# Graph network with gated units on Trainium2: two blocks of the first sum converted ahead of the third layer's weights, and the first normalising blocks placed behind z

## The reference

```python
h = x
for i in range(4):
    hw = einsum('bnc,cd->bnd', h, weight[i])
    m = einsum('bjn,bjd->bnd', adj, hw)
    gx = m @ w_ih[i].T + b_ih[i]
    gh = h @ w_hh[i].T + b_hh[i]
    r = sigmoid(xr + hr);  z = sigmoid(xz + hz)
    n = tanh(xn + r * hn)
    h = (1.0 - z) * n + z * h
y = x + h * mask[:, :, None]
out = (y - mean(y)) / sqrt(var(y) + 1e-5)      # per node, over 128 features
```

## Time and profile before

| | us |
|---|---|
| median of 3 runs | 538.66 (538.38 to 539.0) |
| the profiled execution | 537.98 |
| its span, first to last instruction | 536.2 |
| PE busy in the span | 514.1 (96%), 2288 matmuls |
| DVE busy | 386.1 (72%) |
| ACT busy | 384.6 (72%) |
| POOL busy | 221.2 (41%) |
| granted TensorE clock, mean | 0.990 |

### The profile page before, as it was taken

The page is one execution under the profiler, slowest core; times in us unless marked ns, Lnnn a source line. Parts: engine busy times, 40 slices in busy tenths (PEclk is TensorE's granted clock), DMA queues, the critical chain, the costliest instruction groups (busy, mean ns, idle before and its releaser), DMA issues.

```text
span 536.2 us, 7420 instructions
## 1 busy us (share of the span) xinstructions
PE 514.1 (96%) x2288; PEld 421.5 (79%) x2288; DVE 386.1 (72%) x678; ACT 384.6 (72%) x638; POOL 221.2 (41%) x162
## 2 busy tenths in 40 slices
PE   6999999999999999999999999999999999999970
PEld 4688888888888888888888888888888888888760
DVE  3787666666788886666689886567688887667585
ACT  4668777749776788856886877984986777985444
POOL 2045232344345454432336554232355454344443
PEclk9999999999999999999999999999999999999996
DMA  8941553255732356273662256356472165524212
GB/s 307 382 190 53 213 194 138 91 165 156 238 136 80 122 185 224 82 226 111 198 246 82 65 205 215 117 169 183 137 274 80 60 216 174 185 74 146 90 60 82
DMA packets 78896, 85.13 MB, mean 159 GB/s; under 512 B 3768, under 2 KB 61712, under 8 KB 78864
## 3 DMA queue, kind: packets, MB, share of 16 engines
q1 hardware_dynamic: 78864, 84.73, 47.5%
HBM read 64.27 MB, written 20.45 MB: 158 GB/s over the span
## 4 chain that ended last, share of the span: by engine, by line
PE 92%; DMA 1%; POOL 1%; DVE 1%; issue 1%; SPq 1%; ACT 1%; POOLq 0%; DVEq 0%; ACTq 0%
PE p_S L508 40%; PE p_r L518 6%; PE p_r L522 5%; PE p_r L519 5%; PE p_z L518 5%; PE p_z L522 5%; PE p_z L519 5%; PE p_hn L518 3%; PE p_hn L522 3%; PE p_hn L519 3%; PE p_xn L522 3%; PE p_xn L519 3%; PE p_xn L518 3%; DMA adj_in<-in_adj_dram 1%; PE p_S L478 1%
## 5 line engine op out<-in xcount | busy, mean ns | idle before, releaser
L1272 POOL TENSOR_TENSOR work<-hT,work 128x512 f32<-128x512 f32 x63 | 87.9, 1395 | 266.8 <-ACT work L710 266.8
L508 PE MATMUL p_S<-adj_hi,nat_hi 128*128 128x512 f32 x480 | 187.4, 390 | 0.0
L508 PE MATMUL p_S<-adj_hi,nat_lo 128*128 128x512 f32 x480 | 186.8, 389 | 0.0
L508 PEld LDWEIGHTS p_S<-adj_hi,nat_hi 128*128 128x128 f32 x480 | 90.1, 188 | 18.9 <-DVE nat_lo L894 0.3
L508 PEld LDWEIGHTS p_S<-adj_hi,nat_lo 128*128 128x128 f32 x480 | 90.1, 188 | 18.5
L1141 DVE SCALAR_TENSOR_TENSOR work<-p_hn,bias,work 128x512 f32<-128x512 f32 x62 | 46.5, 750 | 76.2 <-ACT work L710 76.0
L1276 POOL TENSOR_TENSOR work<-work 128x512 f32<-128x512 f32 x63 | 90.1, 1430 | 4.9
L710 ACT ACTIVATE work<-p_r,bsum 128x512 f32<-128x512 f32 x63 | 43.3, 687 | 56.9 <-PE p_r L522 56.2
L931 DVE STREAM_TRANSPOSE work<-hT 128x512 f32<-128x512 f32 x62 | 69.1, 1115 | 2.1
L710 ACT ACTIVATE work<-work,bias 128x512 f32<-128x512 f32 x63 | 45.7, 726 | 31.6 <-DVE work L1145 29.0
L682 ACT ACTIVATE low_words<-adj_in 128x1024 bf16<-128x1024 uint16 x64 | 67.0, 1047 | 1.0
(11 more groups left out here) (148 smaller groups left out, 923.8 us busy)
## 6 DMA issues: line engine op xcount, KB each, us to landing
adj_in<-in_adj_dram SPq DMA_DIRECT2D x72, 512.0 KB, 6.7
bounce<-work SPq DMA_DIRECT2D x62, 256.0 KB, 2.0
low<-bounce SPq DMA_DIRECT2D x62, 256.0 KB, 2.8
x_in<-in_x_dram SPq DMA_DIRECT2D x8, 512.0 KB, 6.8
y<-in_x_dram SPq DMA_DIRECT2D x8, 512.0 KB, 4.4
out_dram<-y SPq DMA_DIRECT2D x7, 512.0 KB, 4.1
out_dram<-y SPq DMA_DIRECT2D x2, 256.0 KB, 2.8
y<-in_L_gnn_w_ih_dram SPq DMA_DIRECT2D x2, 192.0 KB, 7.5
```

The costliest lines, as they stand in the source:

```text
L508: last = nc.tensor.matmul(p_S[h][:, :], part[:, s, j], adj_hi[:, s, j, half(h)], start=(j == 0 and part is nat_hi), stop=(j == NB - 1 and ...
L1272: nc.gpsimd.tensor_tensor(t_sb[:, h], hT[:, s, half(h)], n_sb[:, h], ALU.subtract).then_inc(d_sub, 1)
```

## The change

Three moves, nothing added or removed. On ACT, at the start, the conversion of adjacency block 6 goes from behind `split_joined(2)` to in front of it. On DVE, at the start, `split_weights(2)` goes from in front of `take_odd(0, 7)` to behind `copy_weights(3)`. On ACT, in steps 3 and 4 of pairs 1 to 3, blocks 0 and 1 of the normalising go from `fill(0)` to `fill(1)`.

```diff
                         if g in (3, 4) and not first:
-                            blocks = (range(0, 2), range(0), range(2, 5), range(5, NB))[n]
+                            blocks = (range(0), range(0, 2), range(2, 5), range(5, NB))[n]
                             if len(blocks):
                                 normalise(p - 1, g - 3, blocks)
...
             split_w_hh(1)
             split_joined(1)
             split_w_hh(2)
+            take_adj(0, 0, 6, True)
             split_joined(2)
-            take_adj(0, 0, 6, True)
             split_w_hh(3)
...
             take_odd(0, 5)
             copy_weights(2)
             split_weights(1)
-            split_weights(2)
             take_odd(0, 7)
             copy_weights(3)
+            split_weights(2)
             take_rows()
```

## The result

The changed kernel runs in 537.25 us (median of 21 runs), the kernel before in 538.84 us beside it (21 runs). The ratio is 0.9973 with a 95% interval of 0.9966 to 0.9979, so it is 1.5 us faster (1.1 to 1.8). By the medians the difference is 1.59. Forecast were 537.2 us and 1.5 us less. One execution of the kernel before, timed later beside the experiments, took 1351 us and is left out of every ratio.

The account below looks back on a forecast made before the run. The prediction took TensorE to bound the kernel nearly throughout. Gains of 0.75 at the start and 0.78 in step 4 sum to 1.53 us; 538.66 - 1.5 = 537.2 us, range 536.6 to 538.2.

Parts of the forecast that it names:

- Part 1: Start: ACT converts block 6 earlier, so TensorE takes it 0.77 us sooner; worth 0.75 us, bounds 0.25 to 0.89.
- The links: Start: ACT begins 0 to 0.13 us after block 6 lands, TensorE follows ACT by 0.04, wx_lo finishes before the gates.
- upper bound of 0.89: Start: the gain at block 6 can't exceed 0.89 us, since TensorE isn't free before 20.41.
- tight place: Start, DVE: wx_lo finished at 23.33, first gates at 23.43; 0.06 us left after the signal; up to 0.05 taken off.
- Part 2: Step 4 of pairs 1 to 3: normalising behind z lets r start earlier, closing three TensorE holes of 0.26; 0.78 us.
- nothing comes back from step 3: Step 3 of pairs 1 to 3: TensorE has no hole there, so moving its blocks gains nothing.
- reading row by row: TensorE's timeline: starts not 0.227 us apart showed a hole of 0.26 us in step 4 of pairs 1, 2 and 3.
- The cost put at nothing: Steps 3 and 4: tanh of half 1 up to 0.86 us later, covered by slack; uncovered it would be 5.2 us.
- slack of 1.86: Before the next step's S_lo: 0.82 us of DVE idle time plus 1.04 until TensorE uses S_lo.
- one part only pays: Rival, 537.9 us, chance 0.20: the start's gain is taken back on DVE, or the hole in step 4 stays.
- slower rival: Later tanh of half 1 reaches TensorE at the next S_lo; with table loads around the blocks 546.5 us; chance 0.04.

Follow-up runs that it names:

- Start only: Only the two moves at the start, on ACT and DVE, against the kernel before; normalising unchanged: 537.81 us (538.58 beside it), ratio 0.9975 to 0.9993.
- profile of after: Profile of the changed kernel with all three moves, first run, against the kernel before: 537.25 us (538.84 beside it); profiled execution 537.31 us.
- single moves: ACT's start move without DVE's, and DVE's without ACT's, each against the kernel before: 538.48 and 538.51 us (538.67 beside them).
- z only: Only normalising blocks 0 and 1 moved behind z of half 1 in steps 3 and 4, against the kernel before: 537.97 us (538.58 beside it).
- step 4 only: Kernel before with the two normalising blocks moved behind z in step 4 only, step 3 and start unchanged: 537.87 us (538.78 beside it).
- six blocks: Six normalising blocks instead of two behind z of half 1 in steps 3 and 4, start as before, against the kernel before: 538.68 us (538.67).
- second profile of after: The changed kernel run again without edit, against the kernel before: 536.90 us (538.58 beside it), ratio 0.9968 to 0.9985.
- third profile of after: The changed kernel run a third time without edit, against the kernel before: 537.03 us (538.78 beside it), ratio 0.9944 to 0.9976.

## Why the prediction was right

**Part 1, forecast 0.75.** Start only measured 0.77 by the medians (0.4 to 1.3 by the ratio's interval). The profiles give the part in place, whatever was early or late ahead of it: take the distance on TensorE from the start of layer 3's last transposes (L426) to its first product with block 6. It is 1.37 to 1.39 us in all seven profiles with the old order on ACT, and 0.83, 0.47, 0.76 and 0.73 in the four with both start moves and the old order of loads. So the part was worth 0.55 to 0.91, on average 0.68, where 0.77 was worked out for this place. The links held: ACT started about 0.1 behind the landing or less, TensorE 0.05 behind ACT, and wx_lo was finished 0.13 to 0.29 before the gates, where 0.10 was said (0.06 with the signal).

The forecast kept the landings of one execution, 19.37 for block 6, and in the four profiles it was 19.61 to 20.13. The landing is the last wait in the new order and wasn't in the old one, so the part is worth less when the load is late as seen from TensorE (0.55 in the profile of after) and more when TensorE itself is late (0.91 in the second one). The six profiles under the full old start order have block 6 at 19.34 to 19.77. The change moves nothing that comes earlier, but whether the later landings with it are chance is not shown; nor is why landings differ at all between executions.

The upper bound of 0.89 was misread, since it took the end of the transposes at 20.41 as the earliest start. That end is a modelled one. With block 6 ready the next product starts 0.24 behind the start of L426, so the old distance of 1.38 had 1.14 to give, and 0.91 came in one profile.

**Both moves needed.** The prediction treated split_weights(2) behind ACT's new wait as a tight place. The single moves show that it is a condition: with ACT's alone the gain turns into a wait at block 7.

**Part 2, forecast 0.78.** The stretch fell from 474.55 to 473.78, by 0.77. The times are coarser: z only gives 0.3 by the ratio (0.2 slower to 0.8 faster), step 4 only 1.0 (0.4 to 1.7). The prediction said that nothing comes back from step 3; it didn't say that step 3's move was superfluous, which it is. The mechanism, ACT behind in front of r, is shown by the four orders with eight, eight, six and two blocks in front of it. The reading row by row overlooked other holes on TensorE, which the change doesn't touch: about 0.3 us each near 155 and 417 us, in the profiles of before and after alike.

**The cost put at nothing.** The tanh's delay is 0.65 (forecast 0.6 to 0.9), the new state's 0.39, S_lo's 0.04. The slack of 1.86 was tested with six blocks: at a delay of 1.92 the hole is about 0.1, at 2.09 it is 0.28.

**The rivals.** That one part only pays is excluded by the profiles, where each gain is seen in its own place, and the times agree: by the medians 1.59, 1.68 and 1.75 us with both parts, 0.77, 0.61 and 0.91 with one, though the intervals of single comparisons touch. The profile of after by itself looked like that rival. The slower rival's way by table loads is out: one load, as before, though Identity now stands between Sigmoid and Tanh. The Trainium skill, "ScalarE: Activation LUTs" (Table sets: the hidden batching unit), says that identity is in every set; the trace agrees for the one set that this kernel loads.

**What was luck.** That the total came within 0.1 us of the forecast. Part 1 was 0.07 less in place than forecast and could have been 0.2 less or more with the landings of one execution or another.

**What was not foreseen.** TensorE itself can be the late one at the start, as in the second profile of after. ACT's earlier conversion is then worth more, not less.

## What to carry to other kernels

When a busy engine's wait is to go, ask what is late next, and whether the instruction moved aside heads another engine's queue: here neither move alone showed a gain. Work taken from in front of a critical instruction must leave the whole stretch in which its engine has no idle time, so find where that stretch begins, which here was in the step before. And for changes of a few tenths of a per cent, one profile proves a mechanism by differences inside it (a stretch, a hole), not by its span.

## What the runs showed of the hardware

**TensorE's first stretch has no fixed end.** Matmuls of 512 columns start 0.43 us apart at first, and 0.23 later, with a granted clock of 1.00 listed for either stretch. In the profile of before the spacing changed by 10.65: transposes of layer 0 took 0.49 for three. In that of z only they started at 10.76 and still took 0.84, and the short spacing came only after 12.7:

```profile
9.91 0.63 PE L478 MATMUL p_S<-adj_hi,nat_hi 128*128 128x512 f32 x1
10.34 0.63 PE L480 MATMUL p_S<-adj_hi,nat_lo 128*128 128x512 f32 x1
10.76 0.84 PE L423 MATMUL p_r<-ident,work 128*128 128x128 f32 x3
...
13.02 0.40 PE L478 MATMUL p_S<-adj_hi,nat_hi 128*128 128x512 f32 x1
13.25 0.39 PE L480 MATMUL p_S<-adj_hi,nat_lo 128*128 128x512 f32 x1
```

With landings as early as in before, its gates came 0.72 later. What decides the moment is open.

**One transfer late at the end costs two microseconds.** In the third profile of after, TensorE's last wait for S_lo is 3.2 us instead of 1.2:

```profile
PE p_r L522 <- DVE S_lo L894: 3.2, 1, 3.2
```

DVE's adding of the residual (L947, four adds for each half) stands in front of that S_lo and needs a state on its way back through DRAM. For half 0 the way back, issued at 507.85, took 4.2 us to land, against 2.6 in the profile of before. First the DMA view, then DVE before, then DVE and POOL in the late execution:

```profile
low<-bounce SPq DMA_DIRECT2D x1, 256.0 KB, 4.2
```

```profile
512.48 1.13 DVE L947 SCALAR_TENSOR_TENSOR y<-low,mask,y 128x128 f32<-128x128 f32 x4
```

```profile
512.19 4.45 DVE L947 SCALAR_TENSOR_TENSOR y<-low,mask,y 128x128 f32<-128x128 f32 x4 [0.80 <-DMA low<-bounce]
```

```profile
512.23 1.28 POOL L1272 TENSOR_TENSOR work<-hT,work 128x512 f32<-128x512 f32 x1 [5.07 <-ACT work L710]
```

The wait for the landing itself is only 0.80. The rest is the adds: four took 4.45 instead of 1.13, because three of them now ran beside POOL's three products (from 512.23, 513.58 and 514.95) and took 1.44 to 1.46 each. The adds of half 1, which meet POOL's products in the profile of before (2.72 for four), escaped them here (1.11), and the wait of 0.51 in front of them fell away: 0.80 + 3.32 - 1.61 - 0.51 = 2.0. The way out of half 1 was late too, 3.4 us against 2.0, but it cost nothing: its state was back by 515.57, and its adds started at 517.88.

**An add on DVE takes about four times as long beside a product on POOL.** Over the thirteen profiles there are 728 of these adds of 128x128. The 144 that took 0.58 to 1.46 us all ran beside one of POOL's elementwise instructions for most of their time; the other 584, at about 0.35, overlapped with one for 0.3 us at most. That the one causes the other was not tested by a run of its own. For this kernel it means that a late transfer can cost more than its delay.

That execution took 538.86 us, the other runs of the same kernel beside it 536.56 to 537.40. Single values near 539 stand in several lists of runs, so medians are to be compared here, not means. Why the transfer was late is open.
